# Moving the Gelu groups, the down products and one addition of an overlapped network by one half state in a Mamba, attention and feed-forward stack

## The chip, the core and the metric

The program runs on one core of one Trainium2 chip. The metric is the time of one execution on the device in microseconds (us). Engines are called as the profile calls them: TensorE (PE, its weight loads PEld), VectorE (DVE), ScalarE (ACT), GpSimd (POOL), SyncE (SP, which issues loads and stores).

## What is computed

Four residual layers act on x of shape 4 x 512 x 512, with a context of shape 4 x 512 x 256:

```
x = x + tanh(g_xattn[0]) * mamba(ctx, z = layernorm(x))
x = x + tanh(g_ffn[0])   * bitlinear(gelu(bitlinear(layernorm(x), w1)), w2)
x = x + tanh(g_xattn[1]) * (layernorm(x) @ softmax(q(ctx) k(ctx)^T))
x = x + tanh(g_ffn[1])   * (gelu(layernorm(x) @ proj1^T + b1) @ proj2^T + b2)
```

The mamba layer is a scan over time for each of 512 channels and 16 states: `state = state * dA + (d * u) * b`, `y = sum over states of state * c`. The last network (the fourth line) has 2048 hidden features, and its products are in float32.

## The kernel before

**Passes.** A batch element goes through the scan of layer 1 and then through the rest. The kernel overlaps neighbours: pass 1 runs the scans of element 1 beside the last network of element 0, pass 2 element 2 beside 1, pass 3 element 3 beside 2. A first pass holds the scans of element 0 alone, and a closing part the rest of element 3. So what is said below of a last network beside scans occurs three times.

**Half states and places.** The 16 states of a scan are worked on in halves of two 128-channel tiles: half state s = 2n + p. Their order is cut into slots 4 to 12 (`SCAN_SLOTS`), with four places each: a pair (slot, place). Places (5, 0) to (11, 3) hold one half state each, s = 2 to 29; slot 4 holds s = 0 and 1 in its first two places, slot 12 s = 30 and 31. Every engine has its own instruction list, written out by `pass_`, and the lists meet only in semaphores:

- TensorE in a place broadcasts a row of B or C to all partitions (`scan_bcast`, L443, always into bank 0), then attention products of some places (L511, L455), then its unit of the last network (`f_unit`): an up product (`f_up`, L665) or a pair of down products (`f_down`, L681).
- ScalarE in a place computes the decays of the next half state (`decay_half`, L899, Exp, two tiles), copies the broadcast out of bank 0 (`copy_bc`, L884), then does its small work of the place, then a group of Gelus (`f_gelus`, L1170) where the table has one. Exp and Gelu need different activation tables, so a group stands between two table loads.
- VectorE does the two scans of a half state (L1304) and the product with C (L1311); GpSimd prepares the inputs of a half state four ahead (L1702) and adds half-state results into u by DMA (L1717).

The next broadcast waits until ScalarE has copied the last one (`s_bcc`); the Exp of half state s waits for the product of s - 2 (`s_hc`), since the two share a buffer; the scan waits for the Exp (`s_decay`).

**The last network.** 16 up products f = 0 to 15 fill banks 1, 2, 3 in turn; each is emptied by its Gelu. The down products run in two rounds r = 0 and 1 (two row tiles each, banks 2 and 3 accumulate over f); between them VectorE's `fourth(b, 0)` (L1592) empties the two banks. The order around the change is set by the tables that the diff shows, and these lines give the waits:

```
FFN_UP = {(4 + (f + 3) // 4, (f + 3) % 4): f for f in range(FT)}       L67
f_up:    if f >= 3: pe.wait_ge(s_fgelu, b * FT + f - 2)                 L658
f_down:  r = 1, f = 0: pe.wait_ge(s_x4, b * T + 3)                      L672
         r = 0, f = 0: pe.wait_ge(s_fgelu, b * FT + FT - 1)             L674
f_gelu:  act.wait_ge(s_fmm1, b * FT + f + 1)                            L1169
fourth:  dve.wait_ge(s_fmm2, b * 2 * FT + (r + 1) * FT)                 L1589
```

So up product f waits for Gelu f - 3, which has read the bank that f writes. The up products 3, 6, 9, 12, 15 stand in places (5, 2), (6, 1), (7, 0), (7, 3), (8, 2).

**The turn.** After slot 12, TensorE's `turning` transposes the gated rows (L521), does the last two down pairs, transposes the quantised rows (L532) and goes on with the next element's products (L545). The transposes wait for VectorE's `gated` (L1454).

Of the kernel before, what the change touches and what calls it, by code (L numbers as in the profile page):

```python
# [64 lines left out]
DT_BANKS = (1, 0, 5, 6)  # L65

FFN_UP = {(4 + (f + 3) // 4, (f + 3) % 4): f for f in range(FT)}  # L67
FFN_DOWN = {(8, 3): (0, 0), (9, 0): (0, 2), (9, 1): (0, 4), (9, 2): (0, 6), (9, 3): (0, 8), (10, 0): (0, 10), (10, 1): (0, 12), (10, 2): (0, 14),
            (11, 0): (1, 0), (11, 1): (1, 2), (11, 2): (1, 4), (11, 3): (1, 6), (12, 0): (1, 8), (12, 1): (1, 10)}
FFN_GELUS = {(5, 1): (0, 1, 2), (6, 0): (3, 4, 5), (6, 3): (6, 7, 8), (7, 2): (9, 10, 11), (8, 1): (12, 13, 14), (8, 3): (15,)}  # L70
UP_BANKS = (1, 2, 3)
FOURTH_SLOT = 10


def att_step(slot, which, p, step):

    n = state_at(slot, which)
    if n is None or 2 * n + p < ATT_FIRST + step:
        return None
    j, rest = divmod(2 * n + p - ATT_FIRST - step, ATT_EVERY)  # L80
    return j if rest == 0 and j < J else None


def state_at(slot, which):

    return SCAN_SLOTS[slot][which] if slot in SCAN_SLOTS else None
# [27 lines left out]
def program(nc, x_d, ctxT_d, ipw_d, xpw_d, dtw_d, pch_d, w1_d, w2_d, wqk_d, bqk_d, ffn_d, b1_d, b2_d, gate_d,  # L114
            ident_d, identb_d, pick_d, out_d):
    with ExitStack() as ctx:
# [317 lines left out]
        def _(pe):  # L434
# [222 lines left out]
            def f_up(b, f):  # L657
                if f >= 3:  # L658
                    pe.wait_ge(s_fgelu, b * FT + f - 2)
                elif f == 0:  # L660
                    pe.wait_ge(s_xnTc, b * 2 * T + 2 * T)
                    pe.wait_ge(s_qk, (b + 1) * 2 + 2)
                pe.wait_ge(*loaded(b, f))
                for k in range(J):
                    last = pe.matmul(banks[UP_BANKS[f % 3]][:], piece(b, f)[:, k * P:(k + 1) * P], xnT[:, k, :],  # L665
                                     start=k == 0, stop=k == J - 1)
                last.then_inc(s_fmm1, 1)

            def f_down(b, r, f):
                if f == 0:  # L670
                    if r:
                        pe.wait_ge(s_x4, b * T + 3)  # L672
                    else:
                        pe.wait_ge(s_fgelu, b * FT + FT - 1)  # L674
                elif r == 0 and f == FT - 1:
                    pe.wait_ge(s_fgelu, b * FT + FT)
                k = down_load(r, f)
                block = f if r == 0 else FT - 1 - f
                pe.wait_ge(*loaded(b, k))
                for t in (2 * r, 2 * r + 1):  # L680
                    last = pe.matmul(banks[2 + t % 2][:], h_tile(block)[:, t * P:(t + 1) * P], piece(b, k),  # L681
                                     start=f == 0, stop=f == FT - 1)
                last.then_inc(s_fmm2, 1)

            def f_unit(b, slot, place):
                if (slot, place) in FFN_UP:
                    f_up(b, FFN_UP[slot, place])
                if (slot, place) in FFN_DOWN:
                    r, f = FFN_DOWN[slot, place]
                    f_down(b, r, f)  # L690
# [182 lines left out]
        def _(act):  # L873
# [294 lines left out]
            def f_gelu(b, f):  # L1168
                act.wait_ge(s_fmm1, b * FT + f + 1)  # L1169
                act.activation(h_tile(f), banks[UP_BANKS[f % 3]][:], ACT.Gelu, bias=b1[:, f:f + 1]).then_inc(s_fgelu, 1)  # L1170

            def f_gelus(b, slot, place):
                for f in FFN_GELUS.get((slot, place), ()):
                    f_gelu(b, f)
# [119 lines left out]
        def _(dve):  # L1294
            def half_step(b, n, p, summed):

                s = 2 * n + p
                dve.wait_ge(s_dbu, b * HN + s + 1)
                rows = work[:, s % SCANBUFS, :, :]
                pair = pairs[s % DECAYBUFS]  # L1300
                for q in range(HALF):
                    done = (b * HN + s) * HALF + q + 1
                    dve.wait_ge(s_decay, done)
                    dve.tensor_tensor_scan(pair[:, q, :], pair[:, q, :], rows[:, q, :], 0.0,  # L1304
                                           ALU.mult, ALU.add).then_inc(s_scan, 1)
                if summed is not None:
                    energy_sum(b, summed)
                dve.wait_ge(s_scan, (b * HN + s + 1) * HALF)
                if p == 0:
                    dve.wait_ge(s_bcc, b * 2 * NS + bc_index(n, 1) + 1)  # L1310
                dve.tensor_tensor(rows, pair[:], ccast[:, n % 2, :].unsqueeze(1).broadcast_to([P, HALF, L]),  # L1311
                                  ALU.mult).then_inc(s_hc, HALF)
# [47 lines left out]
            def opening(m):  # L1360

                for j in range(J):
                    convolve(m, j)
                gate_bias()
                split(m)
                step_inputs(m, 0)
                step_inputs(m, 1)

            def between(b, m):

                h_scale(b, 0)
                h_scale(b, 1)
                h_quant(b, 0)
                convolve(m, 0)
                convolve(m, 1)
                h_quant(b, 1)
                convolve(m, 2)
                convolve(m, 3)
                second(b, 0)
                h_scale(b, 2)  # L1380
                h_round(b, 2)
                h_quant(b, 2)
                second(b, 1)
                h_scale(b, 3)
                h_round(b, 3)
                h_quant(b, 3)
                second(b, 2)
                split(m)
                second(b, 3)
                third(b, 0)  # L1390
                step_inputs(m, 0)
                step_inputs(m, 1)
                norm_apply(b, 4)
                third(b, 1)
                norm_apply(b, 5)
                third(b, 2)
                third(b, 3)
# [33 lines left out]
            def half(b, prev, slot, which, p):  # L1431
                if state_at(slot, which) is not None:
                    half_step(b, state_at(slot, which), p, att_step(slot, which, p, 2))
                    energy_max(b, att_step(slot, which, p, 1))

            def energy_max(b, j):
                if j is not None:
                    dve.wait_ge(s_emm, b * J + j + 1)
                    dve.tensor_reduce(ast[:, j, 0:1], banks[1][:], AX.X, ALU.max, negate=True).then_inc(s_emax, 1)
# [100 lines left out]
            def norm_apply(b, i):  # L1540
                t = i % T
                st = fst[:, t, 8:18]
                dve.wait_ge(s_lnrs, b * 2 * T + i + 1)
                if i >= T + 2:
                    dve.wait_ge(s_xnT, b * 2 * T + i - 1)
                dve.tensor_scalar(xn[:, i % 2, :], xb[:, t, :], st[:, 6:7], st[:, 9:10],
                                  ALU.subtract, ALU.mult).then_inc(s_xn, 1)
# [40 lines left out]
            def fourth(b, r):  # L1588
                dve.wait_ge(s_fmm2, b * 2 * FT + (r + 1) * FT)  # L1589
                dve.wait_ge(s_x3b, b * T + T)  # L1590
                for t in (2 * r, 2 * r + 1):
                    dve.scalar_tensor_tensor(xb[:, t, :], banks[2 + t % 2][:], gates[:, 3:4], xb[:, t, :],  # L1592
                                             ALU.mult, ALU.add).then_inc(s_x4, 1)
# [20 lines left out]
            def pass_(b, rest=True):  # L1614

                m, prev = (b + 1, b) if rest else (0, None)
                if rest:
                    dve_f.start()
                dve_m.start()
                if rest:  # L1620
                    between(b, m)
                else:
                    opening(m)
                for slot in range(4, SLOTS):
                    half(m, prev, slot, 0, 0)
                    if rest and slot == 4:
                        norm_apply(b, 6)
                        norm_apply(b, 7)
                    half(m, prev, slot, 0, 1)
                    half(m, prev, slot, 1, 0)  # L1630
                    half(m, prev, slot, 1, 1)
                    if rest and slot == FOURTH_SLOT:
                        fourth(b, 0)
                if rest:
                    turning(b, m)
                else:
                    first_turning(m)

            pass_(None, rest=False)
            for i in range(0, B - 1):  # L1640
                pass_(i)
# [239 lines left out]
```

## Time and profile before

| | us |
|---|---|
| median of 3 runs | 956.47 |
| lowest, highest | 954.84, 959.32 |
| the profiled execution, its own time | 957.99 |
| its span, first to last instruction | 956.2 |
| mean granted TensorE clock | 0.923 of full |

The profile is of one execution. The span leaves out some 1.8 us around the first and the last instruction. TensorE's granted clock is given as a share of full speed: 1.00 is 2.4 GHz, 0.50 is 1.2 GHz. A row in order of time gives start, length, engine, line and operation, and in brackets how long the engine was idle before it and what ended that; "x8" for four float32 matmuls means that each is done in two runs.

### The profile page before, as it was taken

The numbers are of one execution on the slowest core, as the hardware profiler recorded it, in microseconds if no ns is written. First come the engines' busy times: TensorE is split into PE (matmuls) and PEld (weight loads), VectorE is DVE, ScalarE is ACT, GpSimd is POOL, SyncE is SP. The second block draws the span as 40 slices with busy tenths as digits, with TensorE's granted clock in tenths as the row PEclk, the third lists the DMA queues.
The fourth block names the chain that finished last, engine by engine and source line by source line (L and its number), as shares of the span: only waits on it lengthen the run. The fifth ranks groups of instructions, "written<-read, shape, count | busy, mean of one in ns | idle before, by whom it ended". The sixth has DMA issues, their size and how long they took to land. (4 is left out here: it accounts for less than half of the span.)

```text
span 956.2 us, 9268 instructions
## 1 busy us (share of the span) xinstructions
PE 817.1 (85%) x2789; PEld 405.3 (42%) x2789; DVE 778.0 (81%) x905; ACT 647.5 (68%) x975; POOL 520.8 (54%) x425
## 2 busy tenths in 40 slices
PE   6621347999899998999899998998999997898999
PEld 2110023454344444444334444444444444447887
DVE  3899889886899998975989998978899998853333
ACT  5899879774688863773689863775689864623442
POOL 0798794203999881213999891116998861022000
PEclk9755558899999998999999999999999999999999
DMA  8279982001499981301599981301799960201221
GB/s 304 39 146 235 278 160 44 1 1 46 94 222 222 241 190 44 111 0 45 110 219 227 232 192 33 111 1 45 159 219 230 205 177 22 89 1 45 98 101 66
DMA packets 46817, 119.55 MB, mean 125 GB/s; under 512 B 5792, under 2 KB 6944, under 8 KB 46256
## 3 DMA queue, kind: packets, MB, share of 16 engines
q0 software_dynamic: 16128, 58.73, 32.8%
q1 hardware_dynamic: 30640, 60.24, 18.3%
q8 instruction: 22, 0.36, 0.1%
q14 instruction: 27, 0.22, 0.1%
HBM read 56.03 MB, written 4.19 MB: 63 GB/s over the span
## 5 line engine op out<-in xcount | busy, mean ns | idle before, releaser
L1702 POOL TENSOR_TENSOR work<-du,bcast 128x1024 f32<-128x1024 f32 x128 | 358.1, 2872 | 28.2 <-DVE du L1338 28.1
L1304 DVE TENSOR_TENSOR_SCAN pair<-pair,work 128x512 f32<-128x512 f32 x256 | 299.1, 1214 | 20.4 <-ACT pair L899 16.8
L899 ACT ACTIVATE pair<-dt,a_neg 128x512 f32<-128x512 f32 x256 | 165.9, 681 | 30.9 <-DVE work L1311 28.0
L665 PE MATMUL bank<-stage,ring 128*128 128x512 f32 x384 | 176.4, 603 | 2.9 <-ACT stage L1135 2.4
L1311 DVE TENSOR_TENSOR work<-pair,ccast 128x1024 f32<-128x1024 f32 x128 | 156.8, 1225 | 11.5
L1717 POOL DMA_DIRECT2D u<-work x112 | 132.1, 1179 | 39.3 <-DMA u<-work 23.1
L443 PE MATMUL bank<-xd,pick 128*128 128x512 bf16 x128 | 55.2, 431 | 69.4 <-ACT bcast L884 41.8
L665 PEld LDWEIGHTS bank<-stage,ring 128*128 128x128 f32 x384 | 73.5, 193 | 86.8 <-issue 77.3
L1688 POOL TENSOR_SCALAR fst<-fst 128x1 f32<-128x1 f32 x32 | 8.9, 278 | 167.5 <-DVE fst L1538 167.2
L681 PE MATMUL bank<-ring,stage 128*128 128x512 f32 x192 | 88.1, 608 | 0.0
L545 PE MATMUL pair<-w1q,qT 128*128 128x512 bf16 x256 | 62.1, 393 | 5.6 <-ACT qT L1113 5.6
L443 PEld LDWEIGHTS bank<-xd,pick 128*128 128x128 bf16 x128 | 13.0, 101 | 119.6 <-ACT bcast L884 58.1
L884 ACT ACTIVATE bcast<-bank 128x512 f32<-128x512 f32 x64 | 37.5, 586 | 37.2 <-PE bank L443 27.8
L602 PE MATMUL pair<-w2q,hx 128*128 128x512 bf16 x256 | 60.0, 389 | 1.8 <-issue 1.8
L653 PE MATMUL pair<-attT,stage 128*128 128x512 f32 x128 | 57.9, 596 | 0.5 <-ACT stage L1135 0.2
L681 PEld LDWEIGHTS bank<-ring,stage 128*128 128x128 f32 x192 | 37.4, 198 | 42.5 <-issue 42.3
L1319 DVE SCALAR_TENSOR_TENSOR u<-xpad,pch,u 128x512 f32<-128x512 f32 x48 | 40.4, 857 | 11.8 <-ACT u L924 10.7
L681 PE MATMUL bank<-ring,hx 128*128 128x512 f32 x96 | 43.5, 596 | 5.6 <-DVE stage L1592 5.6
L884 ACT ACTIVATE ccast<-bank 128x512 f32<-128x512 f32 x64 | 37.5, 586 | 13.0 <-PE bank L443 12.8
L1135 ACT ACTIVATE stage<-bank 128x512 f32<-128x512 f32 x32 | 18.7, 592 | 38.1 <-PE bank L638 38.0
L1688 POOL TENSOR_SCALAR mst<-mst 128x1 f32<-128x1 f32 x16 | 4.0, 249 | 74.4 <-DVE mst L1503 74.4
L681 PE MATMUL bank<-ring,hT 128*128 128x512 f32 x96 | 43.1, 592 | 0.0
(172 smaller groups left out, 1473.7 us busy)
## 6 DMA issues: line engine op xcount, KB each, us to landing
u<-work POOLq DMA_DIRECT2D x112, 512.0 KB, 6.0
ring<-ffn_dram SPq DMA_DIRECT2D x120, 256.0 KB, 4.7
ring<-ffn_dram SPq DMA_DIRECT2D x16, 512.0 KB, 3.2
xres<-x_dram SPq DMA_DIRECT2D x4, 1024.0 KB, 6.0
stage<-w_dram SPq DMA_DIRECT2D x1, 4096.0 KB, 16.5
stage<-w_dram SPq DMA_DIRECT2D x4, 1024.0 KB, 7.6
out_dram<-stage SPq DMA_DIRECT2D x16, 256.0 KB, 2.1
ctxT<-ctxT_dram SPq DMA_DIRECT2D x4, 512.0 KB, 7.8
```

What stands on the lines that cost most here:

```text
L443: pe.matmul(banks[0][:], pick[:, i * NS + n:i * NS + n + 1].broadcast_to([P, P]), xd3[:], start=True, stop=True).then_inc(s_bc, 1)
L545: last = pe.matmul(banks[4 + g % 3][:], qT[:, k, t * P:(t + 1) * P], w1q[:, k, c * 512:(c + 1) * 512], start=k == 0, stop=k == J - 1)
L602: last = pe.matmul(banks[7][:], hqT[:, f, :], w2q[:, f, :], start=f == 0, stop=f == FT - 1)
L653: last = pe.matmul(banks[ATT_BANKS[t]][:], xnT[:, k, t * P:(t + 1) * P], attT[:, k, :], start=k == 0, stop=k == J - 1)
L665: last = pe.matmul(banks[UP_BANKS[f % 3]][:], piece(b, f)[:, k * P:(k + 1) * P], xnT[:, k, :], start=k == 0, stop=k == J - 1)
L681: last = pe.matmul(banks[2 + t % 2][:], h_tile(block)[:, t * P:(t + 1) * P], piece(b, k), start=f == 0, stop=f == FT - 1)
L884: act.activation(dst[:, n % 2, :], banks[0][:], ACT.Copy).then_inc(s_bcc, 1)
L899: act.activation(pairs[s % DECAYBUFS][:, q, :], dt[:, p * HALF + q, :], ACT.Exp, scale=a_neg[:, p * HALF + q, n:n + 1]).then_inc(s_decay, 1)
L1304: dve.tensor_tensor_scan(pair[:, q, :], pair[:, q, :], rows[:, q, :], 0.0, ALU.mult, ALU.add).then_inc(s_scan, 1)
L1311: dve.tensor_tensor(rows, pair[:], ccast[:, n % 2, :].unsqueeze(1).broadcast_to([P, HALF, L]), ALU.mult).then_inc(s_hc, HALF)
L1702: pool.tensor_tensor(work[:, s % SCANBUFS, :, :], du[:, p * HALF:(p + 1) * HALF, :], bcast[:, n % 2, :].unsqueeze(1).broadcast_to([P, HALF ...
L1717: pool.dma_start(u[:, js, :], work[:, s % SCANBUFS, :, :], accum_op=ALU.add).then_inc(s_acc[p], 16)
```

## The change

Two tables of the last network and the place of one call are changed. Every Gelu group stands one place later on ScalarE; the first round of down products begins at (9, 0) in place of (8, 3), with one pair in every place up to (10, 3); `fourth(b, 0)` stands after the first half state of slot 11, not after the last of slot 10; the second round begins at (11, 1) and not at (11, 0), and its sixth pair stands at (12, 2) in place of (12, 1). The up products stay where they are, and no instruction is added or taken away.

```diff
--- before.py
+++ after.py
@@ -65,11 +65,11 @@
 DT_BANKS = (1, 0, 5, 6)
 
 FFN_UP = {(4 + (f + 3) // 4, (f + 3) % 4): f for f in range(FT)}
-FFN_DOWN = {(8, 3): (0, 0), (9, 0): (0, 2), (9, 1): (0, 4), (9, 2): (0, 6), (9, 3): (0, 8), (10, 0): (0, 10), (10, 1): (0, 12), (10, 2): (0, 14),
-            (11, 0): (1, 0), (11, 1): (1, 2), (11, 2): (1, 4), (11, 3): (1, 6), (12, 0): (1, 8), (12, 1): (1, 10)}
-FFN_GELUS = {(5, 1): (0, 1, 2), (6, 0): (3, 4, 5), (6, 3): (6, 7, 8), (7, 2): (9, 10, 11), (8, 1): (12, 13, 14), (8, 3): (15,)}
+FFN_DOWN = {(9, 0): (0, 0), (9, 1): (0, 2), (9, 2): (0, 4), (9, 3): (0, 6), (10, 0): (0, 8), (10, 1): (0, 10), (10, 2): (0, 12), (10, 3): (0, 14),
+            (11, 1): (1, 0), (11, 2): (1, 2), (11, 3): (1, 4), (12, 0): (1, 6), (12, 1): (1, 8), (12, 2): (1, 10)}
+FFN_GELUS = {(5, 2): (0, 1, 2), (6, 1): (3, 4, 5), (7, 0): (6, 7, 8), (7, 3): (9, 10, 11), (8, 2): (12, 13, 14), (9, 0): (15,)}
 UP_BANKS = (1, 2, 3)
-FOURTH_SLOT = 10
+FOURTH_SLOT = 11
 
 
 def att_step(slot, which, p, step):
@@ -1626,11 +1626,11 @@
                     if rest and slot == 4:
                         norm_apply(b, 6)
                         norm_apply(b, 7)
+                    if rest and slot == FOURTH_SLOT:
+                        fourth(b, 0)
                     half(m, prev, slot, 0, 1)
                     half(m, prev, slot, 1, 0)
                     half(m, prev, slot, 1, 1)
-                    if rest and slot == FOURTH_SLOT:
-                        fourth(b, 0)
                 if rest:
                     turning(b, m)
                 else:
```

**ScalarE, first half of the scans.** Pass 1, around the second Gelu group (up products 3, 4, 5). L899 is the Exp of a half state, bcast and ccast are the copies of broadcasts, L1170 the Gelus. Before:

```order
L899 ACTIVATE pair1<-dt,a_neg 128x512 x2
L884 ACTIVATE bcast<-bank0 128x512
L1170 ACT_TABLE_LOAD
L1170 ACTIVATE stage<-bank1,b1 128x512
L1170 ACTIVATE stage<-bank2,b1 128x512
L1170 ACTIVATE stage<-bank3,b1 128x512
L899 ACT_TABLE_LOAD
L899 ACTIVATE pair0<-dt,a_neg 128x512 x2
L884 ACTIVATE ccast<-bank0 128x512
```

And now:

```order
L884 ACTIVATE bcast<-bank0 128x512
L899 ACTIVATE pair0<-dt,a_neg 128x512 x2
L884 ACTIVATE ccast<-bank0 128x512
L1170 ACT_TABLE_LOAD
L1170 ACTIVATE stage<-bank1,b1 128x512
L1170 ACTIVATE stage<-bank2,b1 128x512
L1170 ACTIVATE stage<-bank3,b1 128x512
L899 ACT_TABLE_LOAD
L899 ACTIVATE pair1<-dt,a_neg 128x512 x2
```

The group now stands behind one more Exp and one more copy: behind the copy of the very broadcast that TensorE issues right before up product 6.

**TensorE, where the down products begin.** Pass 1, places (8, 2) to (9, 1), with one row for a pair of down products:

```order
 L443 MATMUL bank<-xd,pick 128x512
 L665 MATMUL bank<-stage,ring 128x512 x4
-L443 MATMUL bank<-xd,pick 128x512
-L681 MATMUL bank<-ring,stage 128x512 x4
-L443 MATMUL bank<-xd,pick 128x512
-L681 MATMUL bank<-ring,stage 128x512 x4
```

```order
+L443 MATMUL bank<-xd,pick 128x512 x2
+L681 MATMUL bank<-ring,stage 128x512 x4
+L443 MATMUL bank<-xd,pick 128x512
+L511 MATMUL bank<-xpad 128x512
+L681 MATMUL bank<-ring,stage 128x512 x4
```

After the last up product two broadcasts now stand in a row, and the first down pair is behind the second of them; the later pairs follow one place later each.

**VectorE, the addition.** The two additions that empty banks 2 and 3, slots 10 and 11:

```order
 L1311 TENSOR_TENSOR work<-pair,ccast 128x1024
 L1439 TENSOR_REDUCE ast<-bank 128x1
+L1304 SCALAR_TENSOR_TENSOR pair<-pair,work 128x512 x2
+L1530 RECIPROCAL ast<-ast 128x1
+L1311 TENSOR_TENSOR work<-pair,ccast 128x1024
 L1592 SCALAR_TENSOR_TENSOR stage<-bank,gates,stage 128x512 x2
-L1304 SCALAR_TENSOR_TENSOR pair<-pair,work 128x512 x2
-L1530 RECIPROCAL ast<-ast 128x1
-L1311 TENSOR_TENSOR work<-pair,ccast 128x1024
```

Half state 26 is now scanned ahead of the additions.

## Rows read from the trace of the kernel before

**Rows 1.** The page: busy time of the engines over the span (us, share, instructions).
```profile
PE 817.1 (85%) x2789; PEld 405.3 (42%) x2789; DVE 778.0 (81%) x905; ACT 647.5 (68%) x975; POOL 520.8 (54%) x425
```

**Rows 2.** Scan stretches of passes 1 and 3: busy by PE, PEld, DVE, ACT, POOL; clock.
```profile
239.19:365.45 126.26, 120.05 (x304) 52.93 (x303) 117.85 (x110) 100.31 (x164) 111.77 (x74) 0.99 0.84 191
...
706.00:832.00 126.00, 116.10 (x400) 54.84 (x399) 116.69 (x140) 90.55 (x149) 72.46 (x55) 0.99 0.65 157
```

**Rows 3.** VectorE in order of time (start, length, line, operation, idle before), pass 1.
```profile
271.40 1.23 DVE L1311 TENSOR_TENSOR work<-pair,ccast 128x1024 f32<-128x1024 f32 x1
273.18 2.35 DVE L1304 TENSOR_TENSOR_SCAN pair<-pair,work 128x512 f32<-128x512 f32 x2 [0.56 <-ACT pair L899]
...
284.56 2.35 DVE L1304 TENSOR_TENSOR_SCAN pair<-pair,work 128x512 f32<-128x512 f32 x2 [0.57 <-ACT pair L899]
```

**Rows 4.** ScalarE in order of time, one Gelu group and what follows it, pass 1.
```profile
268.97 1.26 ACT L1170 ACTIVATE stage<-bank,b 128x512 f32<-128x512 f32 x2
270.39 0.69 ACT L1170 ACTIVATE stage<-bank,b 128x512 f32<-128x512 f32 x1 [0.15 <-PE bank L665]
271.09 1.28 ACT L899 ACT_TABLE_LOAD   x1
272.39 1.30 ACT L899 ACTIVATE pair<-dt,a_neg 128x512 f32<-128x512 f32 x2
273.63 0.58 ACT L884 ACTIVATE ccast<-bank 128x512 f32<-128x512 f32 x1
```

**Rows 5.** TensorE in order of time, the same stretch.
```profile
266.54 0.38 PE L443 MATMUL bank<-xd,pick 128*128 128x512 bf16 x1
266.75 3.60 PE L665 MATMUL bank<-stage,ring 128*128 128x512 f32 x8
270.19 0.38 PE L443 MATMUL bank<-xd,pick 128*128 128x512 bf16 x1
...
274.26 0.39 PE L443 MATMUL bank<-xd,pick 128*128 128x512 bf16 x1 [0.26 <-ACT ccast L884]
```

**Rows 6.** TensorE, then ScalarE: copies that wait for broadcasts, the load behind one.
```profile
251.51 0.38 PE L443 MATMUL bank<-xd,pick 128*128 128x512 bf16 x1
...
251.92 0.60 ACT L884 ACTIVATE bcast<-bank 128x512 f32<-128x512 f32 x1 [2.08 <-PE bank L443]
...
255.57 0.60 ACT L884 ACTIVATE ccast<-bank 128x512 f32<-128x512 f32 x1 [1.86 <-PE bank L443]
256.19 1.28 ACT L1170 ACT_TABLE_LOAD   x1
257.48 1.27 ACT L1170 ACTIVATE stage<-bank,b 128x512 f32<-128x512 f32 x2
```

**Rows 7.** ScalarE, then TensorE, pass 2: an up product held back by a Gelu.
```profile
482.61 1.84 ACT L1170 ACTIVATE stage<-bank,b 128x512 f32<-128x512 f32 x3
...
483.35 3.70 PE L665 MATMUL bank<-stage,ring 128*128 128x512 f32 x8 [0.58 <-ACT stage L1170]
```

**Rows 8.** TensorE: broadcast of (9, 0), first second-half product, ends of passes 1 and 3.
```profile
312.06 0.38 PE L443 MATMUL bank<-xd,pick 128*128 128x512 bf16 x1
...
343.54 3.70 PE L681 MATMUL bank<-ring,hx 128*128 128x512 f32 x8 [1.88 <-DVE stage L1592]
...
370.13 1.97 PE L521 MATMUL bank<-ident,u 128*128 128x128 f32 x8 [3.55 <-DVE u L1454]
...
372.74 8.63 PE L681 MATMUL bank<-ring,stage 128*128 128x512 f32 x16
381.21 0.39 PE L532 MATMUL bank<-identb,q 128*128 128x128 bf16 x4
...
795.51 7.17 PE L681 MATMUL bank<-ring,stage 128*128 128x512 f32 x16
```

**Rows 9.** TensorE: the first up product of pass 1.
```profile
246.33 5.34 PE L665 MATMUL bank<-stage,ring 128*128 128x512 f32 x8 [0.69 <-ACT stage L1135]
```

**Rows 10.** TensorE by stretch: busy time, granted clock (the 0.50).
```profile
370.00:376.00 6.00, 5.87 (x16) 0.50 0.00 0
```


## The prediction

> **What bounds the kernel now.** I read the page first: TensorE is busy for 85% of the span and VectorE for 81% [rows 1]. No engine is full over the whole, so the shares decide nothing; the change touches only the three scan stretches, and the view by stretch shows both engines near full there, TensorE busy 120 of 126 us, VectorE 118 [rows 2]. Which of the two sets the pace is seen in order of time. VectorE does a half state in 3.58 us (two scans 2.35, the product with C 1.23) and idles 0.56 us ahead of every third one, waiting for an Exp; two such waits are 284.56 - 273.18 = 11.38 us apart [rows 3]. So three half states take 11.38 us, and VectorE is not what holds them.
>
> The reader should now follow the loop. ScalarE's third Gelu of a group starts at 270.39, after 0.15 us of waiting for the up product that has just ended; then come a table load (1.28), two Exps (1.30) and a copy until 274.21 [rows 4]. TensorE's broadcast at 274.26 has waited 0.26 us for that copy, since bank 0 must be empty [rows 5]. From the start of one broadcast to the next TensorE needs 270.19 - 266.54 = 3.65 us for broadcast and up product, and the product starts 0.21 us behind the broadcast [rows 5]. Three times 3.65 is 10.95; the other 0.43 of the 11.38 us is the price of this exchange. TensorE is thus the pacemaker for slots 5 to 8, with hardly any slack, and every idle microsecond put into it there comes out as time.
>
> **The change, part by part.**
>
> *Gelu groups.* Before, Gelu 3 was done in place (6, 0), while TensorE was still in up product 5 of that place; up product 6 of place (6, 1) found its bank empty. Now group 3, 4, 5 stands in place (6, 1), behind the copy of that place's broadcast, and up product 6 stands right behind that broadcast on TensorE and waits for Gelu 3. Nothing can overlap: broadcast, copy, table load, Gelu, up product are one chain. Its links: start of the broadcast to start of its copy 251.92 - 251.51 = 0.41 us; copy to table load 256.19 - 255.57 = 0.62; load to Gelu 257.48 - 256.19 = 1.29 [rows 6]; start of the Gelu to start of the waiting up product 483.35 - 482.61 = 0.74, from the one place where a bank wait already shows [rows 7]. Sum 3.06 us, in place of 0.21: **a stall of 2.85 us**. The three-place loop then is 10.95 + 2.85 = 13.8 us, 2.42 more than now. ScalarE has time for its other work in it (three Gelus 1.84, two loads 2.6, three half states of Exps 3.9, three copies 1.8: 10.1 of 13.8 us), so nothing else grows.
>
> Five up products gate on a moved group: 3, 6, 9, 12, 15. The first stall costs 2.85 in full, the four loops between them 2.42 each: up product 15 starts 12.5 us late. It starts now at 270.19 + 0.21 + 3 x 11.38 = 304.54, then at 317.1.
>
> *Down products.* Place (8, 3) has no product now, which gives time back. The Gelu that frees up product 15 starts at 317.1 - 0.74 = 316.3; ScalarE does three Gelus (1.84), a load and two Exps (2.5) and the copy of (8, 3) (0.6), and the broadcast of (9, 0) follows at 321.3, against 312.06 today [rows 8]: 9.3 us late, 3.2 recovered. The lone sixth Gelu, now in (9, 0), stands beside sums that ScalarE begins there, with its two loads; through the Exp of half state 21 I put that at 0.6 us more. Cover is gone there, but the product of s = 20 on VectorE hides the rest. Pass 1: 9.9. Pass 3 reads alike; in pass 2 one loop holds a bank wait of 0.58 us already [rows 7], so 9.3. Together **+29 us**.
>
> *Weight loads and stores.* SyncE reloads a ring piece when its product is done, so each load for the down products also comes a place later; its use comes a place later too, except in the turn. Between the product that frees the last pair's pieces and that pair lie two other pairs (3.44 each, a place less its broadcast), the transposes (1.97 for the first two) and a further pair, over 12 us still. I cost this, and the stores that follow the additions, at nothing; those 12 us are the cover, and without it TensorE would wait in the turn for what is missing, at most the 3.65 us of one place per pass.
>
> *Additions.* The second round of down products waits 1.88 us for them today [rows 8]. Both sides move by one place; VectorE now does the third half state's 3.6 us first and TensorE a pair (3.44) and the transposes (0.4). The wait stays near 1.5 us: nothing.
>
> *End of a pass.* One more pair (3.44) stands behind slot 12's first. Today TensorE idles 3.55 us before the gate transposes [rows 8]; 0.5 to 0.9 us of that is left, so VectorE still ends the scans. But behind that idle stretch the granted clock was 0.50 for 6 us [rows 10], the 1.2 GHz level, and in pass 1 the 16 runs of the next pairs took 8.63 us, where pass 3 shows 7.17 [rows 8]; the transposes and pairs took 11.1 us to the first quantised transpose. With no long idle stretch the fast clock should last: up to 2.5 us a pass, 7.5 in all, nothing at the other end, since VectorE's own chain is close behind. I take **-4**, the middle.
>
> *Clock of the new stalls.* In a new stall TensorE idles 2.85 less the 0.17 that the broadcast runs beyond its usual overlap, 2.7 us. 3.55 us idle was followed by the 0.50 level, 1.88 us was not: its product took 3.70 us against 3.60 [rows 8]. The stalls are between. An up product at the slow level took 5.34 us against 3.60 [rows 5, 9], so a fall costs 1.74. None of 15 falling is 0, all is 26; 2.7 is the middle of 1.88 and 3.55, so I take half: **+13**. The loop after a fall is paced by TensorE too, so this adds in full.
>
> Sum: 29 + 13 - 4 = **+38 us**. The profiled execution took 957.99, so 996.0; it lies 1.5 above the median of the three runs shown, and I give 994.5 for the median.
>
> The table load is the largest link of the stall. The trace has it at 1.28 us with no gap to speak of on either side: the copy at 255.57 lasts 0.60, the load starts at 256.19 and the Gelu at 257.48 [rows 6]. The Trainium skill (ScalarE: Activation LUTs, section "What ACT_TABLE_LOAD costs") counts a drain of about 1.38 us besides the load for every switch. By that figure each stall would be 4.2 us and the sum, as an estimate from that page, some 59 us; the rows show no such drain, so the measurement stands.
>
> **The rivals.**
>
> *A, every stall takes the clock down.* Speaks for it: the product at 246.33 ran slow after idle stretches much shorter than 3.55, the last 0.69 us, with short work between them [rows 9]. Against: 1.88 us between full products did nothing. Time: 956.5 + 29 + 26 - 4 = 1007.5. [...]
>
> *B, no stall takes it down.* For: the 1.88 us wait. Time: 956.5 + 29 - 4 = 981.5.
>
> *C, the stalls are absorbed.* TensorE idles 3.55 us at a pass's end and VectorE 0.56 per loop; if the scans ran ahead of TensorE by several half states, the five stalls would come out of slack and only that of the turn would change, 955 to 958. Against: ScalarE's Exp and copy alternate in program order, and the copy waits for TensorE's broadcast, so VectorE can be at most about a place ahead.
>
> *D, faster.* If ScalarE, with two more Exps between the groups, were always a place ahead of TensorE, Gelu 3 would be done before up product 6 is due, and the exchange that costs 0.43 us a loop would be gone: 0.43 x 5 loops x 3 passes = 6.5, and with the turn's 4 some 946. It decides from the point where the copy ahead of the group no longer waits for its broadcast. The program order excludes it as I read it, since that copy needs the broadcast that directly precedes the product; only an error of mine in the places would open it.
>
> **How the numbers follow.** Forecast 0.62 (half of the stalls, give or take a few), A 0.14, B 0.18, C 0.03, D 0.03. The likeliest gives 994.5. The range starts below B, since the turn may give back 7.5 and not 4 (978), and ends a little above A, with nothing given back by the turn (1011). A measurement of this kernel tells 0.5%, 4.8 us, from no change: faster 0.03 (D), same 0.03 (C), slower 0.94 (the rest).
>
> **What would show it.** In the profile after: up products 3, 6, 9, 12, 15 with some 2.7 to 2.9 us idle before them, released by ScalarE's L1170, 15 times in all, about 42 us in all, where now one wait of 0.58 stands out; TensorE's 0.26 us waits for a copy gone; VectorE's idle ahead of every third half state at 3 us and not 0.56; loops of 13.8 us, or 15.5 where the clock fell; the stretch of scans ten to fourteen us longer; granted clock 0.50 in slots 5 to 8 for about half of the groups; the idle before the gate transposes under 1 us, and the pairs behind them at 7.0 to 7.2. The argument is wrong if up product 6 does not wait, if the waits are there and the stretch is not longer, or if the turn's gain is missing while its idle stretch is gone.

## The result and the profile after

The changed kernel takes 999.41 us (median of 4 runs, 993.89 to 1000.24), the kernel before 956.88 (954.84 to 959.32): ratio 1.0431, 95% interval 1.0386 to 1.0476. (A ratio is worked out from all runs, so it is not quite the quotient of the medians, here 1.0444. Beside the experiments the kernel before had medians of 959.28 and 958.60 us, and their ratios are against those.) Between the medians lie 42.5 us, where 38 were forecast. The profiled execution took 999.63 us, its span is 997.8 us against 956.2, 41.6 more.

The page of the changed kernel, busy time and two of the costliest groups (busy, mean ns of one, then idle time before them and what ended most of it):

```profile
PE 823.7 (83%) x2749; PEld 404.6 (41%) x2789; DVE 778.5 (78%) x905; ACT 646.6 (65%) x975; POOL 520.7 (52%) x425
L1304 DVE TENSOR_TENSOR_SCAN pair<-pair,work 128x512 f32<-128x512 f32 x256 | 299.2, 1214 | 55.2 <-ACT pair L899 50.8
L665 PE MATMUL bank<-stage,ring 128*128 128x512 f32 x384 | 190.4, 643 | 44.6 <-ACT stage L1170 25.5
```

VectorE, ScalarE and GpSimd do the same work in the same time as before [rows 1]. TensorE is busy 6.6 us longer by the page, but its records are not complete: 2749 matmuls here and 2789 in [rows 1], for the same program; 20 of the 40 missing ones are broadcasts (L443, x108 where the page of before has x128). With the records equal the difference would be larger. The mean of an up product's matmul is 643 ns, 603 before; TensorE's idle time before the up products is 44.6 us. The view of one line adds for L665 what its weight loads and its matmuls waited for (us, times; each wait counts once for a load and once for a matmul):

```profile
  ACT stage L1170: 56.0, 18
  ACT hx L1170: 18.9, 6
  ACT hT L1170: 18.2, 6
```

Thirty waits for a Gelu, so fifteen products, five in each pass. In order of time, TensorE of pass 1: the five products, then the broadcast of (9, 0) and the turn.

```profile
262.65 5.40 PE L665 MATMUL bank<-stage,ring 128*128 128x512 f32 x8 [2.90 <-ACT stage L1170]
...
278.25 5.09 PE L665 MATMUL bank<-stage,ring 128*128 128x512 f32 x8 [2.69 <-ACT stage L1170]
...
293.54 5.40 PE L665 MATMUL bank<-stage,ring 128*128 128x512 f32 x8 [2.90 <-ACT stage L1170]
...
309.14 3.70 PE L665 MATMUL bank<-stage,ring 128*128 128x512 f32 x8 [2.69 <-ACT hT L1170]
...
323.04 3.70 PE L665 MATMUL bank<-stage,ring 128*128 128x512 f32 x8 [2.90 <-ACT hx L1170]
...
327.65 0.39 PE L443 MATMUL bank<-xd,pick 128*128 128x512 bf16 x1 [0.69 <-ACT ccast L884]
...
386.32 1.09 PE L521 MATMUL bank<-ident,u 128*128 128x128 f32 x8 [0.63 <-DVE u L1454]
387.25 0.60 PE L521 MATMUL pair<-ident,u 128*128 128x128 f32 x4
387.69 7.03 PE L681 MATMUL bank<-ring,stage 128*128 128x512 f32 x16
394.56 0.39 PE L532 MATMUL bank<-identb,q 128*128 128x128 bf16 x4
```

Where [rows 5] show the broadcast of (6, 1) right behind the product of (6, 0), with its product due 0.21 us later, each of the five has 2.69 or 2.90 us of idle before it. The stall is the same in both: where 2.90 stands, the profile has no record of the broadcast that ran in between (its copy on ScalarE is there, at 260.00), so 0.21 us more counts as idle. Three took 5.1 to 5.4 us, the other two 3.70; passes 2 and 3 show the same lengths in the same order, so nine of fifteen ran mostly at the slow clock in this execution. The number need not be the same in others: the run of 993.89 us had a mean granted clock of 0.923, the profiled one 0.914. Loops are 15.60 us (262.65 to 278.25), 15.29, 15.60 and, with no slow product in them, 13.90 (309.14 to 323.04), against 11.38. One stall, TensorE's broadcast, ScalarE's copy, load and Gelus:

```profile
275.60 0.60 ACT L884 ACTIVATE ccast<-bank 128x512 f32<-128x512 f32 x1 [1.86 <-PE bank L443]
276.21 1.28 ACT L1170 ACT_TABLE_LOAD   x1
277.51 1.84 ACT L1170 ACTIVATE stage<-bank,b 128x512 f32<-128x512 f32 x3
```

The broadcast started at 275.18, the product at 278.25: 3.07 us. VectorE pays at the next scan, the first row here, and again behind the third stall:

```profile
281.46 2.35 DVE L1304 TENSOR_TENSOR_SCAN pair<-pair,work 128x512 f32<-128x512 f32 x2 [3.91 <-ACT pair L899]
...
296.75 2.34 DVE L1304 TENSOR_TENSOR_SCAN pair<-pair,work 128x512 f32<-128x512 f32 x2 [3.97 <-ACT pair L899]
299.92 1.23 DVE L1311 TENSOR_TENSOR work<-pair,ccast 128x1024 f32<-128x1024 f32 x1 [0.82 <-ACT ccast L884]
```

where [rows 3] had 0.56 and nothing. Behind the two fast products of the pass the wait is 3.07 us, so some 0.8 us of the 3.9 comes with a slow one.

To see where the time went as a whole, I cut the spans of all profiles at two points of every pass: the start of VectorE's first product dt x u (L1338) and of its first closing sum (L1446). Between them lie the scans, from a sum to the next L1338 the turn and what follows it. In us; "turns" are those behind passes 1 and 2, the rest of the span behind the last sum is the tail:

| kernel | scans, passes 1, 2, 3 | turns | tail | span |
|---|---|---|---|---|
| before | 138.9, 138.3, 138.8 | 75.1, 70.6 | 168.0 | 956.2 |
| changed | 154.3, 152.5, 152.5 | 72.8, 72.8 | 165.6 | 997.8 |
| Gelus only | 156.3, 151.4, 154.5 | 71.1, 71.1 | 168.3 | 999.1 |
| down products and addition only | 138.5, 137.8, 138.3 | 69.4, 71.0 | 167.1 | 949.2 |
| changed, Gelus ahead of the copy | 137.0, 136.7, 136.6 | 71.1, 71.1 | 167.0 | 946.2 |
| changed, matmuls in the stalls | 149.6, 147.7, 147.7 | 71.1, 71.1 | 166.8 | 982.2 |
| changed, up products later too | 137.3, 137.3, 136.9 | 72.8, 71.1 | 167.0 | 949.1 |
| one group late | 141.0, 142.1, 142.1 | 72.8, 72.8 | 168.2 | 967.2 |
| copy before Exp | 138.3, 137.7, 137.7 | 72.3, 71.1 | 166.7 | 950.9 |
| copy before Exp, down products and addition moved | 138.1, 137.7, 137.7 | 72.8, 71.1 | 166.4 | 952.3 |

The scans of the three passes grew by 43.3 us, which is the whole loss; turns and tail gave 2.5 back, and 0.8 us came in before the first of these points.

### The profile page after: what moved, and what is told of

The parts are those of the page before. It is cut to its first block and busy times, and to the rows that moved or that the text cites. A ratio compares the mean times of both kernels' runs of the same rounds, so it can differ in the third digit from the quotient of the medians.

```text
span 997.8 us, 9228 instructions
## 1 busy us (share of the span) xinstructions
PE 823.7 (83%) x2749; PEld 404.6 (41%) x2789; DVE 778.5 (78%) x905; ACT 646.6 (65%) x975; POOL 520.7 (52%) x425
## 5 line engine op out<-in xcount | busy, mean ns | idle before, releaser
L1702 POOL TENSOR_TENSOR work<-du,bcast 128x1024 f32<-128x1024 f32 x128 | 348.9, 2790 | 49.9 <-DVE du L1338 28.1
L665 PE MATMUL bank<-stage,ring 128*128 128x512 f32 x384 | 190.4, 643 | 44.6 <-ACT stage L1170 25.5
L899 ACT ACTIVATE pair<-dt,a_neg 128x512 f32<-128x512 f32 x256 | 165.9, 683 | 23.1 <-DVE work L1311 20.1
L1311 DVE TENSOR_TENSOR work<-pair,ccast 128x1024 f32<-128x1024 f32 x128 | 156.8, 1225 | 18.2 <-ACT ccast L884 8.1
L1717 POOL DMA_DIRECT2D u<-work x112 | 126.3, 1128 | 62.3 <-DVE work L1311 42.1
L665 PEld LDWEIGHTS bank<-stage,ring 128*128 128x128 f32 x384 | 77.3, 205 | 142.6 <-issue 87.8
L443 PE MATMUL bank<-xd,pick 128*128 128x512 bf16 x108 | 47.3, 438 | 69.6 <-ACT bcast L884 41.2
L681 PE MATMUL bank<-ring,stage 128*128 128x512 f32 x192 | 85.3, 592 | 0.0
L545 PE MATMUL pair<-w1q,qT 128*128 128x512 bf16 x244 | 59.9, 392 | 7.8 <-ACT qT L1113 6.7
L443 PEld LDWEIGHTS bank<-xd,pick 128*128 128x128 bf16 x128 | 13.0, 101 | 112.7 <-ACT bcast L884 51.3
L681 PEld LDWEIGHTS bank<-ring,stage 128*128 128x128 f32 x192 | 35.9, 190 | 41.3 <-issue 41.2
L1319 DVE SCALAR_TENSOR_TENSOR u<-xpad,pch,u 128x512 f32<-128x512 f32 x48 | 40.5, 858 | 11.7 <-ACT u L924 10.6
L1135 ACT ACTIVATE stage<-bank 128x512 f32<-128x512 f32 x32 | 18.7, 593 | 41.7 <-PE bank L638 41.6
```

The lines of the kernel that those rows point to most:

```text
L545: last = pe.matmul(banks[4 + g % 3][:], qT[:, k, t * P:(t + 1) * P], w1q[:, k, c * 512:(c + 1) * 512], start=k == 0, stop=k == J - 1)
L899: act.activation(pairs[s % DECAYBUFS][:, q, :], dt[:, p * HALF + q, :], ACT.Exp, scale=a_neg[:, p * HALF + q, n:n + 1]).then_inc(s_decay, 1)
L1702: pool.tensor_tensor(work[:, s % SCANBUFS, :, :], du[:, p * HALF:(p + 1) * HALF, :], bcast[:, n % 2, :].unsqueeze(1).broadcast_to([P, HALF ...
L1717: pool.dma_start(u[:, js, :], work[:, s % SCANBUFS, :, :], accum_op=ALU.add).then_inc(s_acc[p], 16)
```

## The experiments

Three theories stood against each other. T: an up product waits for a Gelu that now stands behind the copy of its own place's broadcast, and some of these stalls lower TensorE's clock. U: the down products and the addition cost the time. V: the Gelus stand late against the Exps that VectorE waits for, and TensorE's bank wait is beside the point.

### Each half of the change alone

```diff
-FFN_GELUS = {(5, 1): (0, 1, 2), (6, 0): (3, 4, 5), (6, 3): (6, 7, 8), (7, 2): (9, 10, 11), (8, 1): (12, 13, 14), (8, 3): (15,)}
+FFN_GELUS = {(5, 2): (0, 1, 2), (6, 1): (3, 4, 5), (7, 0): (6, 7, 8), (7, 3): (9, 10, 11), (8, 2): (12, 13, 14), (9, 0): (15,)}
```

> Only the Gelu groups are moved, down products and addition as before. Theory T (up products 3, 6, 9, 12, 15 wait for a Gelu that stands behind a copy, a table load and the broadcast of their own place, 2.85 us each, and some stalls also drop TensorE's clock): the five stalls per pass are there unchanged, 2.7 to 2.9 us of idle each, 15 in all, with 1.74 us more behind those where the clock falls. The empty place (8, 3) is not there to give 3.2 us back, and the idle before the turn stays, so the turn is as slow as before: 1003 us, between 998 and 1010, at or a little above the changed kernel. Rival U (the down products and the addition, a place later, cost the time): within 5 us of 957. Rival V (what costs is that the Exps for VectorE stand behind later Gelus, not TensorE's bank wait): 985 to 1000, but then with no idle before the up products.

Measured: 1000.14 us (997.74 to 1004.47), ratio 1.0441 (1.0395 to 1.0486). The same five stalls a pass, three slow products in pass 1. The Gelus alone make the whole loss; U falls. One part was a miss: the idle before the transposes did not stay at 3.55 us:

```profile
360.76 5.40 PE L681 MATMUL bank<-ring,hx 128*128 128x512 f32 x8 [1.88 <-DVE stage L1592]
...
387.35 1.09 PE L521 MATMUL bank<-ident,u 128*128 128x128 f32 x8 [1.85 <-DVE u L1454]
```

1.85 us, and the transposes behind it ran fast (1.09 us against 1.97 in [rows 8]). The row above it says why: behind 1.88 us of idle the product took 5.40 here and 3.70 in [rows 8], so TensorE reached the turn 1.70 us later, and 3.55 - 1.70 is 1.85. So the same idle time before a product can go either way. So can a stall: with the same idle times, seven of the fifteen products were slow in this profile (three, one and three in the passes), nine in that of the changed kernel.

The other half alone, the changed kernel with the Gelu table of before:

```diff
-FFN_GELUS = {(5, 2): (0, 1, 2), (6, 1): (3, 4, 5), ...
+FFN_GELUS = {(5, 1): (0, 1, 2), (6, 0): (3, 4, 5), ...
```

> Only the down products and the addition are moved, the Gelu groups as before. Theory T: no up product waits; the idle before the gate transposes of the turn falls from 3.55 to under 1 us, the clock stays at the fast level behind it, and from there to the first quantised transpose it takes 8.24 us (as in the changed kernel) in place of 11.08, 9.91 and 9.63: 5.9 us less, 951 us, between 948 and 955. Rival U: 970 to 999. Rival V: as T.

Measured: 952.12 us (950.98 to 952.8), ratio 0.9934 (0.9908 to 0.9961), faster than before. The turn of pass 1:

```profile
370.18 1.09 PE L521 MATMUL bank<-ident,u 128*128 128x128 f32 x8 [0.63 <-DVE u L1454]
```

The idle of 3.55 us is 0.63, as forecast, and the scans are as long as before. So this half of the change is a small gain that the other half buries. The two do not simply add: +42.9 and -7.0 us in the spans would make 35.9, and the changed kernel has 41.6. By the table the difference is in the turns, 72.8 and 72.8 us where each half alone has 69.4 to 71.1; the last section shows which stage it is.

### Cut the link, keep the lateness

In the changed kernel, ScalarE does the group ahead of the copy and the small work of its place (the same for the other three places of a slot; the diff is shortened):

```diff
                     decays(m, prev, slot, 1, 0)
+                    if rest:
+                        f_gelus(b, slot, 2)
                     copy_next(m, slot, 1, 0)
                     quarter(m, slot, 2, rest)
                     attention(m, prev, slot, 1, 0)
-                    if rest:
-                        f_gelus(b, slot, 2)
```

> The changed kernel, but in its place ScalarE does the Gelu group ahead of the copy of the broadcast and not behind it (the Exp stays first). The Gelus are as late as in the changed kernel by places, and the Exps behind them too; only the link to TensorE's own broadcast is cut. Theory T: the chain is now broadcast of the place before, its copy (0.41 + 0.60), Exp 1.24, load 1.29, Gelu start to product 0.74, some 4.3 us against the 3.86 at which the product is due: 0.5 us of stall, loops near 11.4 us, no fall of the clock, total 952 to 960. Rival V: the Exps are as late as before or later, so 985 or more. Rival W (any move of the group behind the Exp of its place costs, by the added 1.3 us of Exp alone): 965 to 975.

Measured: 947.73 us (947.08 to 948.01), ratio 0.9889 (0.9864 to 0.9914). ScalarE around the second group, and then TensorE, the first three of its five products:

```profile
267.82 1.29 ACT L899 ACTIVATE pair<-dt,a_neg 128x512 f32<-128x512 f32 x2
269.13 1.28 ACT L1170 ACT_TABLE_LOAD   x1
270.43 1.85 ACT L1170 ACTIVATE stage<-bank,b 128x512 f32<-128x512 f32 x3
272.15 0.61 ACT L884 ACTIVATE ccast<-bank 128x512 f32<-128x512 f32 x1
```

```profile
259.71 3.70 PE L665 MATMUL bank<-stage,ring 128*128 128x512 f32 x8 [0.45 <-ACT stage L1170]
...
271.17 3.70 PE L665 MATMUL bank<-stage,ring 128*128 128x512 f32 x8 [0.24 <-ACT stage L1170]
...
282.61 3.70 PE L665 MATMUL bank<-stage,ring 128*128 128x512 f32 x8 [0.45 <-ACT stage L1170]
```

The Gelus are in the places of the change and behind the same Exps, and the 2.9 us are 0.45 and 0.24; loops are 271.17 to 282.61 = 11.44 us, products 3.70. V and W (the rival named in the expectation) fall: where the copy stands, behind the group or ahead of it, is worth 51.7 us between the medians. It came out 4 us below the lower end of what I expected, and it is the fastest kernel of this study. The scans are 1.5 to 2.2 us a pass shorter than before the change although the loop is no shorter; what is missing is the wait of the first group, where VectorE idled 2.57 us for its Exp in pass 1 of the kernel before and 0.36 us here.

### Move the up products along

```diff
-FFN_UP = {(4 + (f + 3) // 4, (f + 3) % 4): f for f in range(FT)}
+FFN_UP = {(5 + f // 4, f % 4): f for f in range(FT)}
```

> The changed kernel, with the up products moved one place later as well, so that product, Gelu and down product stand to each other as before the change. Theory T (it is the place of the Gelu group relative to the up product that counts, not how late the Gelus are): no stall of 2.7 to 2.9 us, loops of 11.4 us, the turn as fast as with the down products alone moved (952 us): 952, between 949 and 957. Rival (Gelus that stand later in the scans cost by themselves, against the Exps or the additions): 975 or more.

Measured: 951.37 us (950.92 to 951.69), ratio 0.9933 (0.9911 to 0.9955). TensorE's loop is that of the kernel before, 287.55 - 276.17 = 11.38 us:

```profile
276.17 3.60 PE L665 MATMUL bank<-stage,ring 128*128 128x512 f32 x8
...
287.55 3.60 PE L665 MATMUL bank<-stage,ring 128*128 128x512 f32 x8
```

One product a pass still waits for a Gelu of the first group, 0.59 us in pass 1 and 1.67 in passes 2 and 3. With every part of the network a place later nothing is lost: the distance between product and Gelu counts, not the place.

### The price of the clock

In the changed kernel, TensorE does nine matmuls in each stall whose results are not used:

```diff
             def f_unit(b, slot, place):
+                if (slot, place) in FFN_GELUS and (slot, place) in FFN_UP:
+                    n = state_at(slot, place // 2) + 2 - place % 2
+                    pe.wait_ge(s_bcc, (b + 1) * 2 * NS + bc_index(n, place % 2) + 1)
+                    keep_awake(9, 0)
```

> The changed kernel, with nine matmuls of 0.22 us into bank 0 in each of the 15 stalls, from the moment the broadcast has been copied out of it; the up product still waits for its Gelu. Their results are not used. Theory T with a clock price: the stalls (broadcast to product 3.06 us) stay, the clock no longer falls in slots 5 to 8 (nine falls in the profile of the changed kernel, 1.7 us each: products of 5.09 to 5.40 us in place of 3.70): 999.4 - 15 = 984 us, between 981 and 988. If the fall of the clock costs nothing on the path: 999, no change.

Measured: 983.76 us (982.45 to 983.97), ratio 1.0263 (1.0236 to 1.0289), 15.6 us below the changed kernel. TensorE, one stall:

```profile
274.30 0.38 PE L443 MATMUL bank<-xd,pick 128*128 128x512 bf16 x1
275.37 2.12 PE L476 MATMUL bank<-identb 128*128 128x512 bf16 x9 [0.69 <-ACT ccast L888]
277.37 7.35 PE L665 MATMUL bank<-stage,ring 128*128 128x512 f32 x16
```

The product still starts 3.07 us behind its broadcast, but the two products that follow take 7.35 us together, full speed, in all three passes. The scans of the three passes are 14.3 us shorter than in the changed kernel, and that is what its nine slow products took beyond 3.70 us: six times 1.70 and three times 1.39, together 14.4, or 1.6 each. The other 1.3 us of the 15.6 are not of the stalls: in the table the turns are 3.4 us shorter, the tail 1.2 longer, and the scans of pass 1 begin 0.7 later. What is left is the stalls alone: the scans are 10.7, 9.4 and 8.9 us longer than before the change, 29.0.

### A dose

Against the kernel that has only the down products and the addition moved, the Gelus of one group are moved:

```diff
-FFN_GELUS = {(5, 1): (0, 1, 2), (6, 0): (3, 4, 5), (6, 3): (6, 7, 8), ...
+FFN_GELUS = {(5, 1): (0, 1, 2), (6, 0): (3, 4, 5), (7, 0): (6, 7, 8), ...
```

> Down products and addition moved, and one Gelu group of five, that of up products 6, 7, 8, moved a place later; the other groups as before. A dose test against 952 us with none late. Theory T: three stalls, one a pass, before up product 9, of 2.7 to 2.9 us idle, each 2.4 us on the path and 1.7 more where the clock falls: 952 + 7 to 12, so 959 to 965. If the loss were one effect for the whole set of groups (a lag that is filled once), it would be 952 to 955, or near the whole 47 us.

Measured: 967.29 us (964.96 to 969.01), ratio 1.0091 (1.0064 to 1.0119), 2 us above the range I gave. The profile has the three stalls, one fast and two slow:

```profile
286.55 3.70 PE L665 MATMUL bank<-stage,ring 128*128 128x512 f32 x8 [2.90 <-ACT stage L1170]
...
499.66 5.40 PE L665 MATMUL bank<-stage,ring 128*128 128x512 f32 x8 [2.90 <-ACT stage L1170]
```

In the table the scans are 2.5, 4.3 and 3.8 us longer than with no group late: 10.6 us, which is 3 x 2.4 and 2 x 1.7. So each stall is paid for itself. The profile's span is 18.0 us longer (the medians differ by 15.2): what the scans do not explain lies in the turns (72.8 and 72.8 against 69.4 and 71.0, 5.2 us), in the tail (1.1) and ahead of the scans of pass 1 (1.5), which the moved group does not touch; the last section comes back to that.

### A swap that should shorten the loop of the kernel before

The new function stands in place of the two calls `decays` and `copy_next` in every place from slot 5 on:

```diff
+            def decay_and_copy(b, prev, slot, which, part, rest):
+                place = 4 * slot + 2 * which + part - 1
+                if rest and divmod(place, 4) in FFN_GELUS:
+                    copy_next(b, slot, which, part)
+                    decays(b, prev, slot, which, part)
+                else:
+                    decays(b, prev, slot, which, part)
+                    copy_next(b, slot, which, part)
```

> The kernel before, with two instructions swapped on ScalarE: in the place behind a Gelu group the broadcast is copied out of bank 0 ahead of the table load and the Exps, not behind them. Theory T says that the 11.38 us loop is 10.95 us of TensorE and 0.43 us of waiting for that copy: loops of 10.95 to 11.0 us, TensorE's waits of 0.26 us for a copy gone, 0.43 x 4 loops x 3 passes = 5 us less: 952 us, between 950 and 956. If VectorE's wait for the Exp (0.56 us a loop) is what paces it, the Exp that now comes 0.6 us later makes loops of 11.9 us: 963.

Measured: 954.02 us (952.53 to 954.3), ratio 0.9954 (0.9939 to 0.997): a gain inside the range I gave, but not all by the way I gave: the scans are 0.6, 0.6 and 1.1 us shorter, 2.3 and not 5; the rest of the gain is in turns and tail, which the swap was not meant to change. ScalarE through one loop, and then one row of TensorE (the edit shifts the lines: L1180 is L1170 of the kernel before, L1322 is L1311):

```profile
278.03 1.30 ACT L899 ACTIVATE pair<-dt,a_neg 128x512 f32<-128x512 f32 x2 [1.45 <-DVE work L1322]
279.27 0.58 ACT L884 ACTIVATE ccast<-bank 128x512 f32<-128x512 f32 x1
279.86 1.28 ACT L1180 ACT_TABLE_LOAD   x1
281.16 1.27 ACT L1180 ACTIVATE stage<-bank,b 128x512 f32<-128x512 f32 x2
282.31 0.69 ACT L1180 ACTIVATE hT<-bank,b 128x512 f32<-128x512 f32 x1
282.88 0.61 ACT L884 ACTIVATE bcast<-bank 128x512 f32<-128x512 f32 x1
283.51 1.28 ACT L899 ACT_TABLE_LOAD   x1
284.80 2.52 ACT L899 ACTIVATE pair<-dt,a_neg 128x512 f32<-128x512 f32 x4
```

```profile
281.90 3.70 PE L665 MATMUL bank<-stage,ring 128*128 128x512 f32 x8 [0.26 <-ACT stage L1180]
```

TensorE's wait for the copy is gone, but the loop is 289.30 - 278.03 = 11.27 us, not 10.95, and TensorE waits for a Gelu in it: its product starts 0.43 us behind the broadcast and not 0.21. The loop that sets the pace now is another one: VectorE's product ends, the Exp at 278.03 that waited 1.45 us for it, copy, load, three Gelus, copy, load, the first Exp, VectorE's next scan and the product behind it. It runs over ScalarE and VectorE alone. The kernel before has this loop too, without the second copy in it:

```profile
276.88 1.30 ACT L899 ACTIVATE pair<-dt,a_neg 128x512 f32<-128x512 f32 x2 [0.97 <-DVE work L1311]
278.34 0.60 ACT L884 ACTIVATE ccast<-bank 128x512 f32<-128x512 f32 x1 [0.16 <-PE bank L443]
...
280.25 1.27 ACT L1170 ACTIVATE stage<-bank,b 128x512 f32<-128x512 f32 x2
281.77 0.69 ACT L1170 ACTIVATE hT<-bank,b 128x512 f32<-128x512 f32 x1 [0.26 <-PE bank L665]
282.48 1.28 ACT L899 ACT_TABLE_LOAD   x1
```

There it waits for TensorE twice: from Exp to copy it takes 1.46 us against 1.24 with the swap, from the first Gelu to the third 1.52 against 1.15. Without these 0.59 us it would be 10.8 us long, an estimate. The swap put the copy between the third Gelu and the load, 1.20 us where 0.71 were, and 10.8 + 0.5 is the 11.27 measured. So the swap opened TensorE's loop and lengthened the other one in the same stroke. The run does not speak against the 0.43 us of the exchange; it does not measure it either.

The same edit, with the tables and the call of the kernel with only down products and addition moved:

> The same swap, with the down products and the addition moved as in the change and the Gelus as before. If the two gains are independent (5 us of the loops, 6 to 7 of the turn): 947 us, between 943 and 950, at or below the run with the Gelus ahead of the copy (947.7). If the swap fails, 952 or more.

Measured: 957.75 us over 12 runs (952.62 to 959.23), ratio 0.9985 (0.9965 to 1.0005): no difference from before, and a miss. The scans have kept the swap's length (138.1, 137.7, 137.7), and four of the twelve runs are at 952.6 to 954.1, the profiled one among them, the rest at 957.1 to 959.2. The profile is 3.1 us longer than that of the down products alone: its scans are 1.1 us shorter, but its first turn is 3.4 us longer, and its scans of pass 1 begin 1.5 us later. Why two runs in three are slower still stays open; none of them was profiled.

## Why the prediction was right

- *The bound and the loop.* TensorE paces slots 5 to 8: right for the change, as five stalls a pass came out in full. The other loop, over ScalarE and VectorE (10.8 us by the estimate above), was not looked at; it did not matter here, because the change lengthened the first by 2.4.
- *The stall.* 3.06 us from broadcast to product, 3.07 measured; 2.85 us of stall forecast, 2.86 by these starts, and 2.69 us of idle where the broadcast's record is there, 2.7 forecast. All four links came from rows of the kernel before, [rows 6, 7]. The loop without a slow product is 13.90 us, 13.8 forecast.
- *What the stalls sum to.* 29 us forecast with the 3.2 us that place (8, 3) gives back; 29.0 measured with the clock held up. That the sums agree so well is in part luck: by pass 9.9, 9.3 and 9.9 were forecast, and 10.7, 9.4 and 8.9 came.
- *The clock.* 13 us forecast as half of fifteen falls at 1.74; nine falls at 1.6, 14.3 us, by the scans with and without matmuls in the stalls. Rival B is out, and rival A too: six products ran fast. The size of one fall was read from [rows 5, 9] and is near; the number of falls was a middle between two ends, and that it came near nine is luck. The argument for it, that 2.7 us lies between an idle time of 1.88 that keeps the clock and one of 3.55 that loses it, does not hold: 1.88 us was followed by a slow product with the Gelus alone moved, and of five stalls alike the first three were followed by one and the last two not. What decides stays open.
- *The turn.* -4 us forecast. The mechanism is there: 0.63 us of idle and not 3.55, and 386.32 to 394.56 = 8.24 us for what took 11.1 [rows 8]; in the three turns 8.24 for 11.08, 9.91 and 9.63, so 5.9 us. But turns and tail together are only 2.5 us shorter. The step that was mis-sized is that I counted what the clock gives at the head of the turn and not what it takes behind it: the two turns measure 72.8 and 72.8 us against 75.1 and 70.6, and the second got longer because the clock fell in its stage of L494, 3.3 us (last section).
- *Loads, stores, additions* at nothing: right. The 1.88 us wait for the additions is not in the profile after; TensorE waits 0.69 us for a copy and 0.22 us for attention probabilities just before.
- *The table load without a drain.* The load and Gelu follow at once again (276.21, 277.51), 1.30 us apart, as in [rows 6]; nothing of the drain that the Trainium skill counts for every switch (ScalarE: Activation LUTs, section "What ACT_TABLE_LOAD costs", about 1.38 us) shows in this trace, and the estimate of 59 us from it is not what this chip did here.

In the sum of the spans: stalls 29.0, clock in the scans 14.3, turns and tail -2.5, ahead of the scans of pass 1 0.8, together 41.6, where 29, 13, -4 and nothing were forecast. The mechanism was right and its largest term too; the number of the falls was a guess that came near.

## What to carry to other kernels

When an instruction is moved in one engine's list, write down the semaphore waits of the engine that depends on it and look for an instruction of that same engine that the moved one now stands behind: a wait that closes a chain over two engines costs the whole chain, every time round, and no average shows it coming. One copy on the wrong side of a group of Gelus was worth 51.7 us of 999, and the same groups, in the same places but ahead of the copy, were faster than the original. A change with several parts should be timed in parts; here one part gained 0.7% and the other lost 4.4%.

## What the runs showed that I had not expected

TensorE's clock falls in places that no part of the change touches, and this moves whole stretches in steps of about 1.7 us: the turns of the ten profiles measure 69.4, some 71, 72.8 and 75.1 us. One such place is the stage behind the turn, where the products of 16 rows (L494) stand. By stretch, before the change, in the changed kernel, and then with the down products alone moved (columns as in [rows 2], the clock ahead of the last two):

```profile
427.00:434.00 7.00, 7.00 (x15) 2.17 (x14) 1.26 (x3) 3.20 (x5) 0.57 (x2) 0.51 0.00 0
```

```profile
441.00:448.00 7.00, 6.67 (x15) 2.04 (x15) 1.11 (x3) 2.95 (x5) 0.42 (x2) 0.54 0.00 0
```

```profile
424.00:431.00 7.00, 6.84 (x25) 3.00 (x25) 3.02 (x7) 3.78 (x6) 1.19 (x3) 1.00 0.01 2
```

TensorE counts as busy all through the first, at 0.51 of full speed, the 1.2 GHz level, with the same program in that stage; in the third it was granted all of it. In the changed kernel the stage reads:

```profile
438.62 1.98 PE L494 MATMUL bank<-xd,dtw 16*128 16x512 f32 x4
...
449.05 3.60 PE L653 MATMUL pair<-attT,stage 128*128 128x512 f32 x8
```

From the first row to the second it takes 10.43 us. In the turns of the ten profiles this stretch has three lengths, 7.09, about 8.77 and 10.42 us, and wherever the head of the turn took 8.24 us the whole turn follows them: 69.4, 71.1 and 72.8. The changed kernel has the longest in both turns; the kernel before has 10.43 in its first and 7.09 in its second, which is why the second turn got longer. What decides between the three lengths no run shows.

The same holds for the wait of 1.88 us, once followed by 3.70 us for a product and once by 5.40. In the last kernel of the table a product behind only 0.77 us of idle, with waits of 0.69 and 0.22 us just before, took 5.40 too. Differences of a few microseconds between kernels of this kind, those of the dose test in its turns among them, can come from there, and only a cut of the span by stretch keeps them apart from what a change does.
